# The exponentials of two attentions: maxima as a bias, or subtracted first

## The reference

```
scores = jnp.einsum('bhqd,bkd->bhqk', q, k) / jnp.sqrt(jnp.float32(D_K))
...
scores = jnp.where(causal[None, None], scores, NEG_INF)
attn = jax.nn.softmax(scores, axis=-1)
out = jnp.einsum('bhqk,bkd->bhqd', attn, v)
...
logits = jnp.einsum('bhqd,bhkd->bhqk', q, k) * SCALE
...
logits = logits + bias
attn = jax.nn.softmax(logits, axis=-1)
```

## Time and profile before

| | us |
|---|---|
| median of 3 runs | 1285.19 |
| lowest and highest | 1285.15, 1286.05 |
| span of the profiled execution | 1284.3 |
| TensorE busy in it | 1155.0 (90%) |
| VectorE busy | 946.6 (74%) |
| ScalarE busy | 744.9 (58%) |
| GpSimd busy | 443.5 (35%) |

### The profile page before, as it was taken

How to read it: one execution, slowest core, us unless ns; L and a number is a source line. 1 busy time by engine, 2 the same in 40 slices (tenths; PEclk the granted TensorE clock), 3 DMA queues, 4 the chain that set the end, 5 groups by cost and what they waited for, 6 DMA issues and landing times. The chain is left out here.

```text
span 1284.3 us, 31779 instructions
## 1 busy us (share of the span) xinstructions
PE 1155.0 (90%) x9045; PEld 1104.0 (86%) x9045; DVE 946.6 (74%) x2439; ACT 744.9 (58%) x2297; POOL 443.5 (35%) x656
## 2 busy tenths in 40 slices
PE   7689999999999987999996799999999947767998
PEld 7689999999999987999996699999999837767777
DVE  3567777677776666777776688888888659997656
ACT  3466677567765654333332577677677516666754
POOL 0232222322322210221213454554555346664015
PEclk9889999999999998999998799999999968999559
DMA  7010000000000001000000000000000000000103
GB/s 239 23 67 1 0 0 0 0 0 0 0 0 0 0 2 29 1 0 0 0 0 4 2 1 0 0 0 0 0 0 0 1 18 1 1 0 1 39 27 123
DMA packets 20583, 18.63 MB, mean 15 GB/s; under 512 B 6620, under 2 KB 19644, under 8 KB 20412
## 3 DMA queue, kind: packets, MB, share of 16 engines
q1 hardware_dynamic: 19724, 17.45, 4.3%
q10 hardware_dynamic: 816, 0.66, 0.2%
HBM read 13.89 MB, written 4.19 MB: 14 GB/s over the span
## 5 line engine op out<-in xcount | busy, mean ns | idle before, releaser
L770 POOL TENSOR_TENSOR att_prob<-att_ex,att_rinv 128x308 f32<-128x308 f32 x256 | 179.8, 705 | 326.1 <-DVE att_rinv L651 290.6
L610 ACT ACTIVATE att_ex<-att_s_bank,att_mx 128x77 f32<-128x77 f32 x1024 | 250.2, 334 | 17.1 <-DVE att_mx L641 15.2
L674 DVE TENSOR_TENSOR att_pT_lo<-att_t_bank,att_pT_hi 128x512 fp32r<-128x512 f32 x256 | 176.6, 690 | 50.4 <-ACT att_pT_hi L588 48.1
L486 PE MATMUL att_s_bank<-att_keys,att_qT 128*128 128x154 f32 x1024 | 205.5, 315 | 0.0
L588 ACT CAST att_pT_hi<-att_t_bank 128x512 fp32r<-128x512 f32 x256 | 150.0, 587 | 75.2 <-PE att_t_bank L496 70.3
L510 PE MATMUL att_o_bank<-att_pT_hi,att_vals_hi 128*128 128x256 f32 x512 | 167.5, 327 | 5.1 <-DVE att_pT_lo L674 2.9
L486 PEld LDWEIGHTS att_s_bank<-att_keys,att_qT 128*128 128x128 f32 x1024 | 152.7, 194 | 6.7
L496 PE MATMUL att_t_bank<-all_ident,att_prob 128*128 128x128 f32 x1024 | 152.9, 272 | 0.0
L510 PE MATMUL att_o_bank<-att_pT_lo,att_vals_hi 128*128 128x256 f32 x512 | 144.1, 281 | 0.0
L510 PE MATMUL att_o_bank<-att_pT_hi,att_vals_lo 128*128 128x256 f32 x512 | 143.9, 281 | 0.0
L618 ACT ACTIVATE att_qT<-att_q_bank 128x256 f32<-128x256 f32 x160 | 61.6, 385 | 136.9 <-PE att_q_bank L462 135.9
(11 more groups left out here) (215 smaller groups left out, 3363.0 us busy)
## 6 DMA issues: line engine op xcount, KB each, us to landing
all_x<-in_x SPq DMA_DIRECT2D x4, 1024.0 KB, 8.1
out<-comb_y SPq DMA_DIRECT2D x16, 256.0 KB, 2.1
all_raw<-in_L_ffn_w SPq DMA_DIRECT2D x2, 1024.0 KB, 5.8
moe_w_raw<-in_L_ffn_w SPq DMA_DIRECT2D x32, 64.0 KB, 2.1
pro_ctx_in<-in_ctx SPq DMA_DIRECT2D x4, 308.0 KB
all_raw<-in_L_xattn_W_q SPq DMA_DIRECT2D x1, 1024.0 KB, 8.2
all_raw<-in_L_xattn_W_o SPq DMA_DIRECT2D x1, 1024.0 KB, 10.7
pro_w_raw<-in_L_xattn_w_kv ACTq DMA_DIRECT2D x1, 512.0 KB, 4.8
```

The lines of the kernel that those rows point to most:

```text
L486: last = nc.tensor.matmul(out, qT[c % 2][:, q * P:(q + 1) * P], keys[:, kc, h0:h0 + 2, :], start=first, stop=True)
L610: last = nc.scalar.activation(ex[t % RING][:, r, :], s_bank[t % 2][:, r * SK:(r + 1) * SK], ACT.Exp, bias=mx[t % 2][:, r:r + 1])
L674: nc.vector.tensor_tensor(pT[t % 2][1][:, :], t_bank[t % 2][:, :], fp32_of(pT[t % 2][0][:, :]), ALU.subtract).then_inc(pt_lo, 1)
L770: nc.gpsimd.tensor_tensor(out, e, w, ALU.mult).then_inc(p_ready, 1)
```

## The change

VectorE gets one more instruction a step: `subtract_maxima` takes the four maxima (now not negated) from the 308 scores in PSUM and writes the differences into the ring `ex` in SBUF. ScalarE then takes one exponential of 128x308 in place, without a bias. The scores' bank comes free with the subtraction (`shifted`) and no longer with the exponentials, for TensorE and for `find_maxima`. The waits that guard the ring (`p_ready`, and now also `sum_ready`) move from ScalarE to VectorE.

```
         def exponentials(f, t):
-            act.wait_ge(mx_ready, HP * f + t + 1)
-            at_least(act, p_ready, HP * f + t - RING + 1)
-            for r in range(2 * NC):
-                last = nc.scalar.activation(ex[t % RING][:, r, :], s_bank[t % 2][:, r * SK:(r + 1) * SK], ACT.Exp,
-                                            bias=mx[t % 2][:, r:r + 1])
-            last.then_inc(ex_ready, 1)
+            act.wait_ge(shifted, HP * f + t + 1)
+            nc.scalar.activation(ex[t % RING][:, :, :], ex[t % RING][:, :, :], ACT.Exp).then_inc(ex_ready, 1)
...
         def find_maxima(f, t):
             dve.wait_ge(s_psum, HP * f + t + 1)
-            at_least(dve, ex_ready, HP * f + t - 1)
+            at_least(dve, shifted, HP * f + t - 1)
             nc.vector.tensor_reduce(mx[t % 2][:, :], s_bank[t % 2][:, 0:NC * PAIR].rearrange("p (r k) -> p r k", k=SK), AX,
-                                    ALU.max, negate=True).then_inc(mx_ready, 1)
+                                    ALU.max).then_inc(mx_ready, 1)
+
+        def subtract_maxima(f, t):
+            dve.wait_ge(mx_ready, HP * f + t + 1)
+            at_least(dve, p_ready, HP * f + t - RING + 1)
+            at_least(dve, sum_ready, HP * f + t - RING + 1)
+            nc.vector.tensor_tensor(ex[t % RING][:, :, :], s_bank[t % 2][:, 0:NC * PAIR].rearrange("p (r k) -> p r k", k=SK),
+                                    mx[t % 2][:, :].unsqueeze(2).to_broadcast([P, 2 * NC, SK]), ALU.subtract).then_inc(shifted, 1)
...
                     if front and 1 <= t <= HP:
                         find_maxima(f, t - 1)
+                        subtract_maxima(f, t - 1)
```

More of the change, by code:

```diff
@@ L396, in attention @@
         keys_ready, vals_hi, vals_ready = m.sem("keys_ready"), m.sem("vals_hi"), m.sem("vals_ready")
-        s_psum, mx_ready, ex_ready = m.sem("s_psum"), m.sem("mx_ready"), m.sem("ex_ready")
+        s_psum, mx_ready, shifted, ex_ready = m.sem("s_psum"), m.sem("mx_ready"), m.sem("shifted"), m.sem("ex_ready")
         sum_ready, inv_ready, p_ready = m.sem("sum_ready"), m.sem("inv_ready"), m.sem("p_ready")
@@ L470, in scores @@
                     pe.wait_ge(keys_ready, KC * f + t * KC // HP + 1)
-                at_least(pe, ex_ready, HP * f + t - 1)
+                at_least(pe, shifted, HP * f + t - 1)
                 if t == 0:
@@ L542, in batch @@
                 if back:
-                    pe.wait_ge(ex_ready, HP * f + HP - 1 if front else HP * B)
+                    pe.wait_ge(shifted, HP * f + HP - 1 if front else HP * B)
                     if not front:
```

## The result

The changed kernel takes **1334.45 us** (median of 4 runs, 1333.97 to 1335.13), the kernel before 1285.17 us. The ratio is 1.038, with a 95% interval of 1.037 to 1.040. The span of the profiled execution went from 1284.3 to 1332.6 us, 48.3 us more; the medians differ by 49.3. The forecast was 1330 us, with 44.6 us more.

A forecast was written before the change was run, and what follows sets the result against it. TensorE was taken to bound both attentions, with VectorE near its end in the second. The median before, 1285.2, plus 43.6 (second attention) and 1.0 (first) gave 1329.8, say 1330 us; range 1318 to 1347.

The forecast's parts named there:

- The bound passes to VectorE in the second attention: Second attention: TensorE's step of 1.89 us stays below VectorE's 2.10, so TensorE waits for att_pT_lo.
- The term of 3.06 us a batch: Second attention: eight subtractions add 4.08 us, filled waits take off 1.02; batch grows by 3.06 to 22.2 us.
- 0.51 a step, and the register wait cancels: Second attention, VectorE: step 1.59 becomes 2.10 us; register wait moves from reciprocals to subtraction at no net cost.
- The four waits that I had counted as filled: Second attention, VectorE: waits before att_oT_lo (0.46), att_xT_lo (0.27), att_pT_lo (0.23) and one of 0.06; sum 1.02 us.
- The first attention: First attention: VectorE's 2.44 us step fits TensorE's 2.50; att_oT_lo 0.05 us late 14 times, plus 0.3: 1.0 us slower.
- ScalarE's gain is what pays for the subtraction: First attention: without ScalarE's gain, the 0.45 us wait before att_oT_lo and its like, the subtraction would show.
- the forecast of nothing: Second attention, front-half-only batch: VectorE's 1.49 us step is met by scores no longer waiting for exponentials; no cost.
- Slow waits: Rival, both attentions: every subtraction costs 0.60 us instead of 0.51, from three semaphores or late sums; 1346 us; chance 0.14.
- Clock: Rival, second attention: TensorE's granted clock falls to 0.85, its step becomes 2.16 us, 7 us more: 1337; chance 0.03.
- ScalarE's relief wins: Rival, both attentions: TensorE's waits due to the exponentials go, 6.2 us less: 1279 us; chance 0.03.
- Half: Rival: VectorE finds other waits, such as a subtraction lasting 0.42 us: 1324, or 1314 with the 0.38 bound; chance 0.05.
- hides: Rival, whole kernel: time stays as before, the two effects cancelling: 1285 us; chance 0.03.

The follow-up runs named there:

- two-subtraction kernel: Changed kernel plus, in the second attention, a second subtraction into an unread spare tile ahead of each one: 1384.6 us, ratio 1.077 to the kernel before.

## Why the prediction was right, and where its steps were off

**How near 1330 came.** The span grew by 3.7 us more than forecast. That is the sum of errors with different signs: the second attention cost 7.3 us more than forecast and the first 4.1 less, and the untouched stages moved by 0.5. The mechanism in the second attention was right; that the total is off by only 0.3% is in part luck.

**The bound passes to VectorE in the second attention: right.** The two-subtraction kernel shows it (2.65 us more a batch for 3.1 of VectorE work), and so does the step of 2.10 with TensorE waiting for att_pT_lo. Of the signs that I had named, VectorE "over 93% busy" did not come: it was busy for 89% of a batch, as TensorE was.

**The term of 3.06 us a batch was 0.50 too small.** The step "0.51 a step, and the register wait cancels" held for six steps of eight. The wait did leave the reciprocals (0.50 now where it was 0.59), but ahead of the subtraction it costs 0.65 and 0.77 against 0.50, since three semaphores hang on it; net of the 0.17 that the reciprocals give back this is +0.25 over the two steps. The normalisation, which I left as it was, now falls beside GpSimd's att_prob: +0.23. The four waits that I had counted as filled gave the 1.02 forecast to within 0.01. Together this is 0.48 of the 0.50. Times 13 the 0.50 is 6.5 of the 7.3 us by which the second attention exceeds its forecast.

**The first attention: sign wrong, by 4 us.** I followed VectorE only, and there I was nearly right: the att_oT_lo ahead of the transposes starts 17.35 us after the update of x (246.82 from 229.47), forecast 17.46, before 17.41. What I did not cost is the third place of the diff: the projection's wait, on the exponentials before, on the subtraction now. Before, the seventh of the batch's eight sets of exponentials, for which the projection waits, ended at 249.10 and the projection started at 249.16, 0.52 us after the transposes ahead of it; now it starts 0.36 after them (248.16 to 248.52), at once. That is 0.16 of the 0.24 us a batch; the other 0.07 is att_oT_lo.

**"ScalarE's gain is what pays for the subtraction" there: right in the main, and more than I knew.** Without the gain, and with the bank released by the exponentials, a batch is 28.16 us, where the changed kernel has 26.23. In the second attention's batch with only a front half the forecast of nothing measured 0.4 us more (34.8 instead of 34.4 us from VectorE's first instruction of the stage to its first att_pT_lo), with TensorE waiting up to 1.61 us for the subtraction at 720.05.

**Rivals.** *Slow waits* (0.60 in every step, 1346): the 0.09 appears in no ordinary step; only two steps of eight pay, and more. *Clock* (1337): not at this step of 2.10, but with one subtraction more. *ScalarE's relief wins*: it was priced at 6.2 us and is worth 10; the subtraction costs 59. *Half* and *hides*: the steps exclude both. The prediction gave only half of what the Trainium skill (VectorE: DVE Perf Modes, The DRAIN you can't avoid) says: that a VectorE instruction waits until the one in front has left the pipeline, but also that one that is not held starts earlier. The trace agrees with the second half: behind the 0.48 us subtraction the sums, which need nothing from it, start after 0.39 to 0.40 in every ordinary step. The 0.60 that the prediction put beside the rule was not worked out either: 0.51 to the subtraction and 0.50 instead of 0.38 to the sums would be 0.63.

## What to carry to other kernels

Before work is moved to an engine, read the stage in which that engine has least waiting left, step by step: the same edit was free in one attention, where TensorE's step is 2.50 us and ScalarE gave time back, and cost 3.6 us a batch in the other. Idle time counts only at the place where the new work stands, and what an edit takes off another engine counts only where somebody waits for it. Go through every changed wait of a diff, not only the instructions.

## What the runs showed of the hardware that I had not expected

- The two normalisations of 128x256 took 0.98 us with a GpSimd multiplication that had started 0.19 us before them, and 0.73 without; the first of the two took all of the extra time (0.66 against 0.40). In the kernel before an overlap existed too, but began later in GpSimd's instruction, and cost little (0.77):

```profile
833.59 0.77 DVE L324 TENSOR_SCALAR att_xn<-all_x,att_mean_var,att_rstd 128x256 f32 x2
```

```profile
833.18 0.70 POOL L770 TENSOR_TENSOR att_prob<-att_ex,att_rinv 128x308 f32<-128x308 f32 x1 [1.01 <-DVE att_rinv L651]
```

- A wait of a VectorE instruction that goes through a register instruction costs 0.09 us with two semaphores (0.59) and 0.15 to 0.27 with three (0.65 and 0.77); without it two and three cost the same (0.50).
- Four exponentials of 128x77 take 0.98 us from PSUM with a bias, 0.74 from SBUF without one; one of 128x308 without a bias takes 0.46 from SBUF and 0.44 from PSUM.
- With waits of about 1.2 and 0.9 us one after the other in every batch, TensorE's granted clock halved for some 3.5 us behind them in two batches of five, and not in the others.
